# The loop's turned attention heads go through the ring of three banks of transposed scores instead of the ring of four banks of row scores

## The reference

```python
xn = layernorm(x)
q, k = rope(xn @ wq + bq), rope(xn @ wk + bk); v = xn @ wv + bv     # 32, 8 and 8 heads of 16
probs = softmax(einsum("bqhd,bkhd->bhqk", q, repeat(k, 4)) / sqrt(16))   # all 1024 keys, no mask
s = einsum("bhqk,bkhd->bqhd", probs, repeat(v, 4))
z = xn @ W.T + b;  m = sum over e of p[e] * (xn @ A[e]) @ B[e]
gate = silu(z + min(0.5 * norm(z) / (norm(m) + 1e-6), 1) * m)
out = x + s * gate
```

## Time and profile before

| | |
|---|---|
| median of 3 runs | 427.78 us |
| the profiled execution's own time | 427.93 us |
| its span, first to last instruction | 426.1 us |
| TensorE (PE) busy | 410.3 us, 96% |
| VectorE (DVE) busy | 356.6 us, 84% |
| ScalarE (ACT) busy | 333.6 us, 78% |
| GpSimd (POOL) busy | 189.2 us, 44% |
| mean granted TensorE clock | 0.986 of full speed |

### The profile page before, as it was taken

How to read it: one execution, slowest core, us unless ns; L and a number is a source line. 1 busy time by engine, 2 the same in 40 slices (tenths; PEclk the granted TensorE clock), 3 DMA queues, 4 the chain that set the end, 5 groups by cost and what they waited for, 6 DMA issues and landing times.

```text
span 426.1 us, 8603 instructions
## 1 busy us (share of the span) xinstructions
PE 410.3 (96%) x3215; PEld 195.0 (46%) x3215; DVE 356.6 (84%) x643; ACT 333.6 (78%) x653; POOL 189.2 (44%) x243
## 2 busy tenths in 40 slices
PE   7999989989999999999999999999999999999994
PEld 3556545655434344444444443444444343454441
DVE  5862677775999999999999999999999999933553
ACT  2445354574899998999989898999999999976884
POOL 7979972548444230403142043314332455501555
PEclk9999999995999999999999999999999999999999
DMA  8959995544610020000000000000000030002002
GB/s 263 306 119 127 130 135 75 77 75 75 190 37 3 0 58 3 3 3 0 3 2 4 1 3 3 2 4 0 4 2 3 1 102 2 4 2 88 25 22 68
DMA packets 15449, 21.51 MB, mean 50 GB/s; under 512 B 3328, under 2 KB 7712, under 8 KB 15408
## 3 DMA queue, kind: packets, MB, share of 16 engines
q1 hardware_dynamic: 13888, 19.85, 22.6%
q10 hardware_dynamic: 1520, 1.12, 1.0%
HBM read 10.13 MB, written 2.10 MB: 29 GB/s over the span
## 4 chain that ended last, share of the span: by engine, by line
PE 84%; POOL 6%; ACT 4%; DVE 3%; issue 2%; DMA 1%; DVEq 0%; ACTq 0%; POOLq 0%
PE st L1501 33%; PE oT L1469 27%; PE oT L1556 3%; PE sm L1581 3%; PE st L1248 2%; PE sm L1478 2%; PE oT L1248 2%; PE st L1535 2%; PE sm L1394 2%; PE sm L1369 1%; POOL arena L591 1%; PE oT L1442 1%; POOL x_low_parts L602 1%; DVE relus L1069 1%; POOL qA L595 1%
## 5 line engine op out<-in xcount | busy, mean ns | idle before, releaser
L1081 DVE TENSOR_REDUCE half_top<-sm 128x1 f32<-128x512 f32 x448 | 271.0, 680 | 4.2 <-PE sm L1369 3.6
L979 ACT ACTIVATE arena<-st 128x512 f32<-128x512 f32 x448 | 233.0, 600 | 25.4 <-PE st L1501 20.5
L1369 PE MATMUL sm<-kA,qA 48*128 48x512 f32 x448 | 157.4, 446 | 1.4 <-DVE row_top L1069 1.4
L1501 PE MATMUL st<-qA,kA 50*128 50x512 f32 x448 | 155.3, 442 | 0.1
L1469 PE MATMUL oT<-arena,vg 128*32 128x256 f32 (+3 forms) x1568 | 128.5, 419 | 0.1
L1501 PEld LDWEIGHTS st<-qA,kA 50*128 50x128 f32 x448 | 74.0, 186 | 97.7 <-ACT arena L979 80.8
L718 POOL TENSOR_TENSOR rsum<-junk,consts 128x16 f32<-128x16 f32 x13 | 37.9, 2915 | 101.2 <-ACT junk L947 101.2
L1369 PEld LDWEIGHTS sm<-kA,qA 48*128 48x128 f32 x448 | 74.0, 186 | 3.2 <-DVE row_top L1069 2.1
L1469 PEld LDWEIGHTS oT<-arena,vg 128*32 128x32 f32 x1568 | 33.5, 108 | 46.1 <-issue 42.5
L1069 DVE CUSTOM_DVE_ANT_0 relus<-sm,relus 128x512 f32<-128x512 f32 x32 | 21.4, 687 | 19.9 <-ACT relus L849 16.3
L1004 ACT ACTIVATE arena<-st 128x512 f32<-128x512 f32 x48 | 26.9, 601 | 9.4 <-PE st L1535 9.4
(11 more groups left out here) (193 smaller groups left out, 483.0 us busy)
## 6 DMA issues: line engine op xcount, KB each, us to landing
qA<-arena SPq DMA_DIRECT2D x45, 128.0 KB, 4.6
x_sb<-in_x SPq DMA_DIRECT2D x16, 256.0 KB, 3.8
wT_sb<-in_wT SPq DMA_DIRECT2D x2, 1024.0 KB, 7.0
kA<-qA SPq DMA_DIRECT2D x12, 128.0 KB, 6.7
out<-x_sb SPq DMA_DIRECT2D x1, 896.0 KB, 4.3
out<-x_sb SPq DMA_DIRECT2D x4, 224.0 KB, 2.0
z_sb<-in_wq SPq DMA_DIRECT2D x1, 768.0 KB, 10.0
B_sb<-in_B SPq DMA_DIRECT2D x2, 256.0 KB, 7.1
```

Source lines behind the costliest of these rows:

```text
L979: act.activation(probs[:, s % PB, h, :], st[:, st_score(0, s, h) % 3, :], ACT.Exp, scale=float(D) ** -0.5).then_inc(st_free, 1)
L1081: dve.tensor_reduce(half_top[:, e // 16, e % 16, j % 2:j % 2 + 1], sm[:, n % 4, :], AX.X, ALU.max).then_inc(sm_free, count)
L1369: pe.matmul(sm[:, n % 4, :], qA[rows, half, g // 2, h, qt * P:(qt + 1) * P], kA[rows, g // 2, kh * HALF:(kh + 1) * HALF], start=True, stop ...
L1501: pe.matmul(st[:, n % 3, :], kA[rows, g // 2, kt * P:(kt + 1) * P], qA[rows, half, g // 2, h, :], start=True, stop=True).then_inc(st_full, 1)
```

## The change

The turned heads become two uses of the `st` ring (`st_out1`, `st_out0`), between the scores of steps 17 and 18 and of 49 and 50. `ST_PER` becomes 68 and `SM_PER` 64. TensorE waits for a free bank of that ring before it turns; ScalarE copies out of that bank, and its copy counts on `st_free`, like the exponentials. VectorE's maxima count one each, the semaphore `turned_out` and the two waits for it are gone, and GpSimd waits on `st_free` in its place. In group 0, which has no turn at step 18, the product and the exponential of step 17 count two. As 68 is no multiple of 3, the `st` bank of a step now differs from pass to pass, so the banks are named by the running number; after the loop the four banks of `last_bank`, `BANK_C`, `BANK_Z` and `BANK_M` follow from that. The first late product of tile 4 then waits for row score 61 of the last pass and that of tile 5 for 62, where both waited for 62.

```diff
-ST_PER, SM_PER = 66, 66
+ST_PER, SM_PER = 68, 64
 def st_score(g, s, h):
     i = 4 * s + h
-    return ST_PER * g + i + (i >= MAX1_AT) + (i >= MAX0_AT)
+    return ST_PER * g + i + sum(i >= at for at in (MAX1_AT, OUT1_AT, MAX0_AT, OUT0_AT))
...
+def st_out1(g):
+    return ST_PER * g + OUT1_AT + 1
+def st_out0(g):
+    return ST_PER * g + OUT0_AT + 3
...
 def sm_score(g, j):
-    return sm_base(g) + j + (1 if j >= OUT1_AT else 0) + (1 if j >= OUT0_AT else 0)
+    return sm_base(g) + j
...
-BANK_C, BANK_Z, BANK_M = 2, (3, 0), 1
+BANK_C, BANK_Z, BANK_M = 0, (1, 2), 3
...
-                pool.wait_ge(turned_out, n + 1)
+                pool.wait_ge(st_free, (st_out1((n + 1) // 2) if n % 2 else st_out0(n // 2)) + 1)
...
             def copy_turned(n, at):
-                act.wait_ge(sm_full, at + 1)
+                act.wait_ge(st_full, at + 1)
                 act.wait_ge(heads_scaled, n)
-                act.activation(turned, sm[:, at % 4, :], ACT.Copy).then_inc(turned_out, 1)
+                act.activation(turned, st[:, at % 3, :], ACT.Copy).then_inc(st_free, 1)
...
-                        act.activation(probs[:, s % PB, h, :], st[:, st_score(0, s, h) % 3, :], ACT.Exp,
-                                       scale=float(D) ** -0.5).then_inc(st_free, 1)
+                        act.activation(probs[:, s % PB, h, :], st[:, st_score(g, s, h) % 3, :], ACT.Exp,
+                                       scale=float(D) ** -0.5
+                                       ).then_inc(st_free, 2 if first and 4 * s + h == OUT1_AT - 1 else 1)
...
-                    row_max(g, j, 2 if j in (OUT1_AT - 1, OUT0_AT - 1) else 1)
+                    row_max(g, j)
...
                     pe.matmul(st[:, n % 3, :], kA[rows, g // 2, kt * P:(kt + 1) * P], qA[rows, half, g // 2, h, :],
-                              start=True, stop=True).then_inc(st_full, 1)
-                    if i == OUT1_AT + 3 and not first:
-                        pe.wait_ge(turned_out, 2 * g)
-                    if i == OUT0_AT + 3:
-                        pe.wait_ge(turned_out, 2 * g + 1)
-                    score_rows(g + 1, i, sm_score(g, i), 2 if first and i == OUT1_AT - 1 else 1)
+                              start=True, stop=True).then_inc(st_full, 2 if first and i == OUT1_AT - 1 else 1)
+                    score_rows(g + 1, i, sm_score(g, i))
...
                     if i == OUT1_AT - 1 and not first:
-                        pe.wait_ge(sm_free, sm_out1(g) - 3)
-                        turn_heads(1, sm[:, sm_out1(g) % 4, :], 2 * g).then_inc(sm_full, 1)
+                        pe.wait_ge(st_free, st_out1(g) - 2)
+                        turn_heads(1, st[:, st_out1(g) % 3, :], 2 * g).then_inc(st_full, 1)
...
-                        pe.wait_ge(sm_free, sm_score(LAST - 1, 62) + 1)
+                        pe.wait_ge(sm_free, sm_score(LAST - 1, 61 + t - TH) + 1)
```

More of the change, by code:

```diff
@@ L122, in st_max0 @@
 def st_max0(g):
-    return ST_PER * g + MAX0_AT + 1
+    return ST_PER * g + MAX0_AT + 2
+def st_out1(g):
+    return ST_PER * g + OUT1_AT + 1
+def st_out0(g):
+    return ST_PER * g + OUT0_AT + 3
 def block_parts(b):
@@ L345, in last_bank @@
         def last_bank(n):
-            return sm[:, BANK_C, :] if n % LAST_RING == 3 else st[:, n % LAST_RING, :]
+            if n % LAST_RING == 3:
+                return sm[:, BANK_C, :]
+            return st[:, (st_score(LAST - 1, 15, 1) + n % LAST_RING) % 3, :]
         def pj(n):
@@ L382, in build @@
             "heads_out", "sums_inv", "heads_scaled", "heads_gated", "group_done"))
-        turned_out = sem("turned_out")
         dense3_full, dense3_free = sem("dense3_full"), sem("dense3_free")
@@ L952, in step @@
                         if 4 * s + h == OUT1_AT and not first:
-                            copy_turned(2 * g - 1, sm_out1(g))
+                            copy_turned(2 * g - 1, st_out1(g))
                         if 4 * s + h == OUT0_AT:
-                            copy_turned(2 * g, sm_out0(g))
+                            copy_turned(2 * g, st_out0(g))
                         if 4 * s + h == MAX1_AT:
@@ L959, in step @@
                                 act.wait_ge(max_in, 16 * 2 * g)
-                            act.activation(maxT[:, 1, :], st[:, st_max1(0) % 3, :].bitcast(BF16)[0:32, 0:P],
+                            act.activation(maxT[:, 1, :], st[:, st_max1(g) % 3, :].bitcast(BF16)[0:32, 0:P],
                                            ACT.Copy).then_inc(st_free, 1)
@@ L964, in step @@
                             act.wait_ge(max_in, 16 * (2 * g + 1))
-                            act.activation(maxT[:, 0, :], st[:, st_max0(0) % 3, :].bitcast(BF16)[0:32, 0:P],
+                            act.activation(maxT[:, 0, :], st[:, st_max0(g) % 3, :].bitcast(BF16)[0:32, 0:P],
                                            ACT.Copy).then_inc(st_free, 1)
@@ L987, in step @@
                         if (s, h) == (1, 1) and not first:
-                            evacuate(blocks_through(g - 1, 2 * NT - 1), 1, (sm_full, sm_out1(g - 1) + 1))
+                            evacuate(blocks_through(g - 1, 2 * NT - 1), 1, (st_full, st_out1(g - 1) + 1))
                         if (s, h) == (9, 1):
-                            evacuate(blocks_through(g, NT - 1), 0, None if first else (sm_full, sm_out0(g - 1) + 1))
+                            evacuate(blocks_through(g, NT - 1), 0, None if first else (st_full, st_out0(g - 1) + 1))
             step(0, first=True)
@@ L1006, in _ @@
                 if s == 1:
-                    evacuate(2 * BLOCKS * LAST, 1, (sm_full, sm_out1(LAST - 1) + 1))
+                    evacuate(2 * BLOCKS * LAST, 1, (st_full, st_out1(LAST - 1) + 1))
                 if s == NT + 1:
-                    evacuate(last_values(NT - 1), 0, (sm_full, sm_out0(LAST - 1) + 1))
+                    evacuate(last_values(NT - 1), 0, (st_full, st_out0(LAST - 1) + 1))
                 if s in (7, 10, 13):
@@ L1075, in first_row_max, with row_max @@
                 top_of_sum(row_top[:, e // 16, e % 16:e % 16 + 1], sm[:, (2 * e + 1) % 4, :], e).then_inc(sm_free, 2)
-            def row_max(g, j, count):
+            def row_max(g, j):
                 n, e = sm_score(g, j), j // 2
@@ L1081, in row_max @@
                 dve.tensor_reduce(half_top[:, e // 16, e % 16, j % 2:j % 2 + 1], sm[:, n % 4, :], AX.X,
-                                  ALU.max).then_inc(sm_free, count)
+                                  ALU.max).then_inc(sm_free, 1)
             def both_halves(g, half):
@@ L1360, in _, with score_rows @@
             pe.wait_ge(wq_put, 2 * CHUNKS)
-            def score_rows(g, j, n, count):
+            def score_rows(g, j, n):
                 e, kh = j // 2, j % 2
@@ L1369, in score_rows @@
                 pe.matmul(sm[:, n % 4, :], qA[rows, half, g // 2, h, qt * P:(qt + 1) * P],
-                          kA[rows, g // 2, kh * HALF:(kh + 1) * HALF], start=True, stop=True).then_inc(sm_full, count)
+                          kA[rows, g // 2, kh * HALF:(kh + 1) * HALF], start=True, stop=True).then_inc(sm_full, 1)
             entries = iter(range(32))
@@ L1488, in group @@
                         pe.wait_ge(st_free, st_max1(g) - 2)
-                        turn_maxima(st[:, st_max1(0) % 3, :], 1).then_inc(st_full, 1)
+                        turn_maxima(st[:, st_max1(g) % 3, :], 1).then_inc(st_full, 1)
                     if i == MAX0_AT:
@@ L1492, in group @@
                         pe.wait_ge(st_free, st_max0(g) - 2)
-                        turn_maxima(st[:, st_max0(0) % 3, :], 0).then_inc(st_full, 1)
+                        turn_maxima(st[:, st_max0(g) % 3, :], 0).then_inc(st_full, 1)
                     if i % (REP * NT) == 0:
@@ L1518, in group @@
                     if i == OUT1_AT - 1 and not first:
-                        pe.wait_ge(sm_free, sm_out1(g) - 3)
-                        turn_heads(1, sm[:, sm_out1(g) % 4, :], 2 * g).then_inc(sm_full, 1)
+                        pe.wait_ge(st_free, st_out1(g) - 2)
+                        turn_heads(1, st[:, st_out1(g) % 3, :], 2 * g).then_inc(st_full, 1)
                     if i == OUT0_AT - 1:
-                        pe.wait_ge(sm_free, sm_out0(g) - 3)
-                        turn_heads(0, sm[:, sm_out0(g) % 4, :], 2 * g + 1).then_inc(sm_full, 1)
+                        pe.wait_ge(st_free, st_out0(g) - 2)
+                        turn_heads(0, st[:, st_out0(g) % 3, :], 2 * g + 1).then_inc(st_full, 1)
             def last_scores(s):
```

## The result

The changed kernel takes 430.0 us (median of 21 runs, 425.79 to 431.63) against 427.78 us (median of 21 runs, 423.65 to 430.22): a ratio of 1.0058, 95% interval 1.0034 to 1.0082. In us the interval is 1.5 to 3.5, and 2.1 were forecast. Its profiled execution took 430.05 us with a span of 428.2, against 427.93 and 426.1.

The account below looks back on a forecast made before the run. TensorE was taken to set the pace at the turn, with VectorE uncovered at step 21. Thirteen turns at 0.17 us, 2.2, less 0.1 in pass 0, gave 2.1 us: median 429.9 us, forecast's own range 428.6 to 430.2, whole range 427.7 to 430.6.

Parts of the forecast that it names:

- The pace: At the turn: TensorE sets the pace, VectorE has no cover for step 21, so TensorE's delay there delays the loop equally.
- The turn's own wait, steps 18 and 19: Turn moved to the transposed ring, next two steps with one bank less ahead: cost 0; VectorE's 0.11 us loss stays.
- Step 20: Its transposed score waits for ScalarE's copy, values come later: 0.17 us a turn, 2.2 us over 13 turns.
- Pass 0, step 18: No turn here, the skipped use moves to the other ring: a gain of 0.1 us, between 0 and 0.2.
- The rest: ScalarE's copy place, GpSimd's release, SP's waits, VectorE's instructions and the last group's late products: 0.
- Weights loaded meanwhile: Rival at step 20: loads go ahead during the wait, restart 0.33, shift 0.07 a turn, 428.6 us; chance 0.09.
- Taken up later: Rival: TensorE's later waits for ScalarE shrink by what the turn adds, time stays at 427.7 us; chance 0.11.
- Dearer: Rival: step 19's margin of 0.02 fails too, burst restarts twice, 0.10 more a turn, 431.2 us; chance 0.04.
- Faster: Rival at step 20: row score stops waiting for VectorE, copy's end not felt, −0.09 a turn, 426.6 us; chance 0.06.

Follow-up runs that it names:

- the wait alone: Kernel before, turned heads still in the row-score ring, transposed scores of steps 20 and 52 also wait for ScalarE's copy: 430.33 us, ratio 1.0073.
- the shorter copy: Changed kernel, ScalarE copies only the 17 of 32 columns of each head that GpSimd reads: 426.06 us, ratio 0.9969.
- the mended wait: Kernel before, at steps 20 and 52 the wait for ScalarE's copy replaces the bank's own count, one wait, not two: 428.47 us, ratio 1.0035.
- the 25 columns: Changed kernel, ScalarE copies 25 of 32 columns of each head: 424.9 us, measured once.

## Why the prediction was right

- **The pace.** TensorE leads at the turn, VectorE has no cover at step 21: shown. With the wait alone the pass lengthens by as much as in the changed kernel, and copies of three lengths carry over one to one. That nothing made the delay up has another reason than the one I gave, TensorE's own pace: away from the turns it is VectorE that has no time to spare.
- **The turn's own wait, steps 18 and 19:** 0 forecast. The pitch from 17 to 18 stayed at 0.71 and the loads of the two steps are 0.10 us apart (192.28, 192.38), with nothing lost ahead of step 20.
- **Step 20:** 0.05 from the copy's end to the load and 0.43 to the values, as taken from the held load of the earlier trace rows; 0.17 us a turn forecast, 0.17 measured (0.34 a pass). The row of 0.43 was the right one to take, as here too load and product start together.
- **Pass 0, step 18:** a gain of 0.1 forecast. The values there come at 114.86, not at 114.96; both executions had begun that burst within 0.01 us of each other.

```profile
114.86 0.16 PEld L1471 LDWEIGHTS oT<-arena,vg 128*32 128x32 f32 x8 [0.37 <-ACT arena L980]
```

- **The rest:** span 428.2 forecast and measured; from the last joining to the end it is 50.9 us in both kernels. That the two agree to the tenth has some luck in it, as the stretch at 97 us was equally long in both executions.
- **The rivals.** Weights loaded meanwhile: no, 0.43 and not 0.33. But this rival was drawn from a wrong reading: its 0.33 counts from a product's start (190.36), the 0.43 of the earlier trace rows from a load's, and the load ahead of that product was held as well, until 190.26. The two figures differ by the load's lead over its own product, not by what was loaded behind it. Taken up later: no, the pass keeps the whole delay. Dearer: no. Faster: not in this change, and the shorter copy showed that its price was set too high. I had −0.09 a turn once the bank is free by the time the product runs; freed at that time, it gave −0.02 (1.61 to 1.59), as the load has to start some 0.1 us before. Whether an earlier release would bring the rest was not tried: the copy cannot start before the turn ends.

Of the versions tried, the changed kernel with the 17-column copy has the shortest pass, 0.04 us under the kernel before, some 0.3 us over the loop. The ratio of times, 0.9969 with an interval that ends at 0.9999, holds also the chance length of the slow stretch; I do not call it a proven gain.

## What to carry to other kernels

A buffer's place in a ring is not free because somebody else's ring has fewer waits: ask which later use will want that bank, and when its reader starts and ends. A wait put into the list of an in-order engine costs what it delays the next engine that has nothing in hand: here 0.17 us a turn out of an idle of 0.46. If that engine is full everywhere else, the delay is not made up. And a wait that ends just when the product could run is still late, by what its load would have run ahead, here 0.1 us.

## What the runs showed of the hardware

- A weight load held by a semaphore was not overtaken: in the changed kernel the row score's load, which needs no more than VectorE's maximum of step 16 (VectorE went on to step 17 at 192.14), started only at 193.04, behind the held load at 193.03.
- The next block's loads start 0.42 to 0.44 us after such a load. Counted from the product it is 0.43 where the load starts with it and 0.33 where it started 0.1 us ahead.
- From the end of ScalarE's copy to the load that it releases took 0.05 us at all 13 turns, in the changed kernel and with the mended wait alike.
- A second semaphore on a load moved its start from 0.05 to 0.12 us after the release.
- ScalarE's copy from PSUM took 0.41 us for 272 elements a row, 0.52 for 400 and 0.60 for 512.
- TensorE ran at a granted clock of 0.50 (1.2 GHz) after it had been partly idle from 92 us on, for 10.2 us in the profiled executions of the kernels before and after, for 3.4 us with the mended wait and not at all with the 25 columns. In the stretches 92 to 95, 95 to 98, 98 to 102 and 102 to 106 us the clock (third number from the end) is, first in the changed kernel, then with 25 columns:

```profile
92.00:95.00 3.00, 2.52 (x13) 1.34 (x9) 2.96 (x7) 1.63 (x5) 1.19 (x1) 1.00 0.72 85
95.00:98.00 3.00, 1.82 (x6) 0.65 (x6) 3.00 (x8) 2.73 (x6) 2.17 (x5) 0.77 0.23 72
98.00:102.00 4.00, 4.00 (x11) 2.64 (x12) 1.30 (x4) 0.65 (x3) 2.96 (x7) 0.50 1.05 137
102.00:106.00 4.00, 4.00 (x12) 2.31 (x12) 2.21 (x4) 2.00 (x4) 3.73 (x4) 0.50 0.08 8
```

```profile
92.00:95.00 3.00, 2.48 (x13) 1.35 (x9) 2.96 (x7) 1.59 (x5) 1.20 (x1) 1.00 0.70 83
95.00:98.00 3.00, 1.62 (x7) 0.64 (x7) 3.00 (x8) 2.76 (x6) 2.17 (x5) 1.00 0.23 71
98.00:102.00 4.00, 4.00 (x20) 2.52 (x20) 3.12 (x6) 2.52 (x6) 2.97 (x7) 1.00 1.05 137
102.00:106.00 4.00, 4.00 (x32) 1.62 (x31) 3.92 (x7) 3.48 (x9) 3.83 (x4) 1.00 0.10 16
```

TensorE's work ahead of that stretch is nearly the same in both. So a change of half a per cent in this kernel is better read from the passes than from the total.
